# Folding two separate stages of an eight-core RWKV-style layer into the blocks beside them

## What is computed

```
xn = layernorm(x)
xx = shift(xn) - xn                                # the token before, minus this one
xk, xv, xr, xg = xn + xx * tm_k, tm_v, tm_r, tm_g
k = xk @ Wk.T;  v = xv @ Wv.T;  r = xr @ Wr.T;  g = sigmoid(xg @ Wg.T)
wkv = scan over tokens of (a + e^u e^k v) / (b + e^u e^k)
o = (sigmoid(r) * wkv * g) @ Wo.T
s = layernorm(o) * ln_g + ln_b
scale = mean(abs(Wf));  w_t = clip(round(Wf / scale), -1, 1)
g2 = silu(xn @ (w_t * scale).T + bias)
y = x + s * g2
```

## Time and profile before

| what | us |
|---|---|
| median of two timed runs (1721.29, 1731.93) | 1726.61 |
| the profiled execution, device time | 1707.37 |
| its span on the slowest core (3) | 1705.8 |
| spans of the eight cores | 1696.6 to 1705.8 |
| TensorE busy | 815.9 (48% of the span) |
| VectorE busy | 600.4 (35%) |
| ScalarE busy | 461.9 (27%) |
| mean granted TensorE clock, core 3 | 0.742 |

### The profile page before, as it was taken

How to read it: one execution, slowest core, us unless ns; L and a number is a source line. 1 busy time by engine, 2 the same in 40 slices (tenths; PEclk the granted TensorE clock), 3 DMA queues, 4 the chain that set the end, 5 groups by cost and what they waited for, 6 DMA issues and landing times. The chain is left out here.

```text
span 1705.8 us, 12040 instructions; the slowest of 8 cores (1696.6 to 1705.8 us)
## 1 busy us (share of the span) xinstructions
PE 815.9 (48%) x3834; PEld 363.1 (21%) x3834; DVE 600.4 (35%) x977; ACT 461.9 (27%) x605; POOL 118.1 (7%) x190
## 2 busy tenths in 40 slices
PE   0520000421494948999950767709466029884000
PEld 0100000000252424544420323304223014331000
DVE  0059993001101000467104454446553320001844
ACT  0810001421221212122112334443334422445400
POOL 0002221000010000001110000000000010000010
PEclk9955555555797978999985888859788559987555
DMA  6003333775526374465127444463544462300076
GB/s 196 27 32 129 144 146 141 258 230 176 174 108 188 120 250 142 144 220 176 59 77 226 128 131 135 131 198 111 166 134 142 121 165 70 116 1 0 0 252 240
DMA packets 86910, 238.91 MB, mean 140 GB/s; under 512 B 11584, under 2 KB 15680, under 8 KB 84800
## 3 DMA queue, kind: packets, MB, share of 16 engines
q1 hardware_dynamic: 52128, 139.57, 27.8%
q0 software_dynamic: 20896, 76.56, 13.0%
q10 hardware_dynamic: 13824, 22.03, 3.8%
HBM read 180.44 MB, written 53.48 MB: 137 GB/s over the span
## 5 line engine op out<-in xcount | busy, mean ns | idle before, releaser
L963 PE MATMUL rgo_ps<-mov_rg,rgo_wbf 128*128 128x512 bf16 x1024 | 237.6, 397 | 204.3 <-ACT rgo_wbf L780 67.0
L379 PE MATMUL g1ps<-mov_kv,g1wbf 128*128 128x512 bf16 (+1 forms) x1536 | 261.1, 335 | 140.1 <-ACT g1wbf L246 60.1
L780 ACT ACTIVATE rgo_wbf<-rgo_mw 128x512 bf16<-128x512 f32 x192 | 119.6, 629 | 309.1 <-DMA rgo_mw<-wr 111.4
L379 PEld LDWEIGHTS g1ps<-mov_kv,g1wbf 128*128 128x128 bf16 x1536 | 132.9, 101 | 268.2 <-issue 152.9
L963 PEld LDWEIGHTS rgo_ps<-mov_rg,rgo_wbf 128*128 128x128 bf16 x1024 | 103.2, 101 | 338.8 <-issue 228.6
L963 PE MATMUL rgo_ps<-wkv_sb,rgo_wbf 128*128 128x512 bf16 x512 | 117.5, 394 | 84.2 <-ACT rgo_wbf L780 76.6
L621 PE MATMUL ps_sc<-fs_a,ones 128*1 128x512 f16 x64 | 29.8, 621 | 216.9 <-ACT fs_a L609 216.9
L244 DVE CAST g1wbf<-g1mwstg 128x1024 bf16<-128x1024 f32 x32 | 22.2, 694 | 271.7 <-DMA g1mwstg<-wk 96.2
L379 PE MATMUL g1ps<-xn_sb,g1wbf 128*128 128x512 bf16 x512 | 112.4, 383 | 5.6 <-DVE g1wbf L241 5.6
L308 ACT ACTIVATE g1row<-g1ps 128x512 f32<-128x512 f32 (+1 forms) x96 | 44.8, 492 | 147.5 <-PE g1ps L379 132.6
L963 PEld LDWEIGHTS rgo_ps<-wkv_sb,rgo_wbf 128*128 128x128 bf16 x512 | 51.4, 101 | 150.3 <-issue 94.5
(11 more groups left out here) (120 smaller groups left out, 882.7 us busy)
## 6 DMA issues: line engine op xcount, KB each, us to landing
fs_w<-wf SPq DMA_DIRECT2D x16, 1024.0 KB, 6.0
g1mwstg<-wk SPq DMA_DIRECT2D x32, 512.0 KB, 5.2
g1mwstg<-wv SPq DMA_DIRECT2D x32, 512.0 KB, 5.1
g1mwstg<-wf SPq DMA_DIRECT2D x32, 512.0 KB, 4.7
rgo_mw<-wr SPq DMA_DIRECT2D x64, 256.0 KB, 3.5
rgo_mw<-wg SPq DMA_DIRECT2D x64, 256.0 KB, 3.4
rgo_mw<-wo SPq DMA_DIRECT2D x64, 256.0 KB, 3.2
x_sb<-x SPq DMA_DIRECT2D x16, 576.5 KB, 15.2
```

The source lines that it names most:

```text
L379: mm = e.matmul(bank[:, :t1 - t0], wbf[hh % 2][:, ic, oc * 128:(oc + 1) * 128], s["mov"][:, ic, t0:t1], start=(ic == 0), stop=(ic == CH - 1))
L780: e.activation(wbf[ss % 2][:, ic, :], mwstg[jj % 2][:, :], AF.Copy).then_inc(sem["scs"], 1)
L963: mm = e.matmul(bank[:, :t1 - t0], wbf[ss % 2][:, ic, oc * 128:(oc + 1) * 128], phs[p]["mov"][:, ic, t0:t1], start=(ic == 0), stop=(ic == ...
```

## The change

The scale stage loses its block. Its SP, ACT, PE and DVE work is written into block B of the first layer norm: SP's loads first thing there, ACT's and PE's part behind their broadcasts, DVE's five small operations behind its 16 chunks. Two semaphores are exchanged (`scv` for `ss`, `srd` for `sv`).

The last stage loses its block too. Its work is written into block B of the second layer norm. `s_sb` goes; ACT writes a double tile `sstg`, and DVE does the normalisation of chunk `ci`, then multiply and add of chunk `ci - 1`. The tiles for x, g2 and y are double as before.

Cut to its core:

```diff
@@ block B of the first layer norm
+            QC = _tchunks(C)
+            nbc = len(TC_STG)
@@ its tensor stream, behind the pb1 and pb2 matmuls
+                for ic in range(CH):
+                    e.wait_ge(sem["scv"], b["scv"] + ic + 1)
+                    for j, (q0, q1) in enumerate(QC):
+                        mm = e.matmul(ps_sc[:, :q1 - q0], ones16[:, :],
+                                      habs[ic % 2][:, q0:q1],
+                                      start=(ic == 0 and j == 0),
+                                      stop=(ic == CH - 1 and j == len(QC) - 1))
+                    inc(mm, "smm")
+                e.wait_ge(sem["srd"], b["srd"] + 1)
...
+            @blk.sync
+            def _(e):
+                for ic in range(CH):
+                    if ic >= 2:
+                        e.wait_ge(sem["scv"], b["scv"] + ic - 1)
+                    inc(e.dma_start(wstg[ic % 2][:, :],
+                                    w_d["wf"][ic * 128:(ic + 1) * 128, :]),
+                        "sw%d" % (ic % 2), 16)
@@ its scalar stream, behind rb_sb and m2b_sb
+                for ic in range(CH):
+                    swp = "sw%d" % (ic % 2)
+                    e.wait_ge(sem[swp], b[swp] + 16 * (ic // 2 + 1))
+                    if ic >= 2:
+                        e.wait_ge(sem["smm"], b["smm"] + nbc + ic - 1)
+                    inc(e.activation(habs[ic % 2][:, :], wstg[ic % 2][:, :],
+                                     AF.Abs), "scv")
+                e.wait_ge(sem["smm"], b["smm"] + nbc + CH + 1)
+                e.activation(scale_sb[:, :], ps_bc[:, 0:1], AF.Copy)
...
@@ its vector stream, behind the 16 chunks
+                e.wait_ge(sem["smm"], b["smm"] + nbc + CH)
+                e.tensor_copy(sctile[:, :], ps_sc[:, :])
...
+                inc(e.tensor_scalar(sctiny[:, 2:3], sctiny[:, 1:2], -1.0, None,
+                                    OP.mult), "srd")
@@ the scale stage's own block
-    with contextlib.ExitStack() as es:
...
@@ block B of the second layer norm
-    s_sb = s_es.enter_context(nc.sbuf_tensor("s_sb", [128, CH, T_OWN], F32))
+            @blk.sync
+            def _(e):
+                for ci in range(CH):
+                    if ci >= 2:
+                        e.wait_ge(sem["sden"], b["sden"] + ci - 1)
+                    inc(e.dma_start(xst[ci % 2][:, :],
+                                    x_d[ci * 128:(ci + 1) * 128,
+                                        1 + LANE:T_STG]),
+                        "sw%d" % (ci % 2), 16)
+                    inc(e.dma_start(g2ld[ci % 2][:, :], sg2[ci, :, :]),
+                        "sw%d" % (ci % 2), 16)
             @blk.scalar
                 for ci in range(CH):
                     e.wait_ge(sem["sv"], b["sv"] + ci + 1)
-                    inc(e.activation(s_sb[:, ci, :], ost[ci % 2][:, :],
+                    if ci >= 2:
+                        e.wait_ge(sem["sden"], b["sden"] + ci - 1)
+                    inc(e.activation(sstg[ci % 2][:, :], ost[ci % 2][:, :],
+            def final_part(e, ci):
+                swp = "sw%d" % (ci % 2)
+                e.wait_ge(sem["ss"], b["ss"] + ci + 1)
+                e.wait_ge(sem[swp], b[swp] + 32 * (ci // 2 + 1))
+                if ci >= 2:
+                    stp = "st%d" % (ci % 2)
+                    e.wait_ge(sem[stp], b[stp] + 16 * (ci // 2))
+                e.drain()
+                e.tensor_tensor(outst[ci % 2][:, :], sstg[ci % 2][:, :],
+                                g2ld[ci % 2][:, :], OP.mult)
+                e.drain()
+                inc(e.tensor_tensor(outst[ci % 2][:, :], outst[ci % 2][:, :],
+                                    xst[ci % 2][:, :], OP.add), "sden")
@@ its vector stream, in the loop over ci
                     inc(e.tensor_tensor(ost[ci % 2][:, :], ost[ci % 2][:, :],
                                         m2b2[:, :], OP.subtract), "sv")
+                    if ci >= 1:
+                        final_part(e, ci - 1)
+                final_part(e, CH - 1)
+            @blk.gpsimd
+            def _(e):
+                for ci in range(CH):
+                    e.wait_ge(sem["sden"], b["sden"] + ci + 1)
+                    inc(e.dma_start(y_d[ci, :, :], outst[ci % 2][:, :]),
+                        "st%d" % (ci % 2), 16)
...
@@ the last stage's own block
-    with contextlib.ExitStack() as es:
-        ec = es.enter_context
-        xst = [ec(nc.sbuf_tensor("xst%d" % i, [128, T_OWN], F32))
```

More of the change, by code:

```diff
@@ L509, in build_nc @@
             pb2 = ecB(nc.psum_tensor("pb2", [128, 512], F32))
+            SCW = min(512, C)
+            ps_sc = ecB(nc.psum_tensor("ps_sc", [1, SCW], F32))
+            ps_bc = ecB(nc.psum_tensor("ps_bc", [128, 4], F32))
+            wstg = [ecB(nc.sbuf_tensor("fs_w%d" % i, [128, C], F32))
+                    for i in range(2)]
+            habs = [ecB(nc.sbuf_tensor("fs_a%d" % i, [128, C], F16))
+                    for i in range(2)]
+            sctile = ecB(nc.sbuf_tensor("sctile", [1, SCW], F32))
+            sctiny = ecB(nc.sbuf_tensor("sctiny", [1, 4], F32))
             blk = esB.enter_context(nc.Block())
             b = snap()
+            QC = _tchunks(C)
+            nbc = len(TC_STG)
             @blk.tensor
@@ L564, in _ @@
                         "sv")
+                e.wait_ge(sem["smm"], b["smm"] + nbc + CH)
+                e.tensor_copy(sctile[:, :], ps_sc[:, :])
+                e.drain()
+                e.reduce_sum(sctiny[:, 3:4], sctile[:, :], axis=AX.X)
+                e.drain()
+                e.tensor_scalar(sctiny[:, 0:1], sctiny[:, 3:4], 1.0 / (C * C),
+                                None, OP.mult)
+                e.drain()
+                e.tensor_scalar(sctiny[:, 1:2], sctiny[:, 0:1], FFN_EPS, 0.5,
+                                OP.add, OP.mult)
+                e.drain()
+                inc(e.tensor_scalar(sctiny[:, 2:3], sctiny[:, 1:2], -1.0, None,
+                                    OP.mult), "srd")
             @blk.gpsimd
@@ L972, in build_nc @@
     o_sb = sr_sb
-    s_es = contextlib.ExitStack()
-    s_sb = s_es.enter_context(nc.sbuf_tensor("s_sb", [128, CH, T_OWN], F32))
     with contextlib.ExitStack() as es:
@@ L1049, in build_nc @@
             pb2 = ecB(nc.psum_tensor("qb2", [128, 512], F32))
+            sstg = [ecB(nc.sbuf_tensor("sstg%d" % i, [128, T_OWN], F32))
+                    for i in range(2)]
+            xst = [ecB(nc.sbuf_tensor("xst%d" % i, [128, T_OWN], F32))
+                   for i in range(2)]
+            g2ld = [ecB(nc.sbuf_tensor("g2ld%d" % i, [128, T_OWN], BF16))
+                    for i in range(2)]
+            outst = [ecB(nc.sbuf_tensor("outst%d" % i, [128, T_OWN], F32))
+                     for i in range(2)]
             blk = esB.enter_context(nc.Block())
             b = snap()
+            ntc2 = len(TC_OWN)
             @blk.tensor
```

118 lines of the change are left out of this document (13 added, 105 removed).

## The result

The changed kernel takes 1618.35 us (median of 11 runs, 1611.7 to 1627.6), the kernel before, run beside it, 1726.61 us (median of 10, 1706.1 to 1759.0). The ratio is 0.9445, 95% interval 0.9409 to 0.9481: faster by 5 to 6%. The forecast was 1610 us, the range 1588 to 1640. The time lies 8.4 us above the forecast and inside the range.

A forecast was written before the change was run, and what follows sets the result against it. Stages that leave idle what their neighbour needs stand one behind the other only because all engines meet between blocks. 75.1 + 39.3 - 3 = 111.4 us, taken from 1721.3, gives 1610 us; range 1588 to 1640.

The forecast's parts named there:

- The last stage, +39.3: Folded into the second layer norm's block B: 16 chunks of 5.30 us, last add at 1661.4 instead of 1700.7, gain 39.3 us.
- the slack of 0.7 and 0.9 us: Last stage: 8.07 us of DVE work was to cover g2's load (7.35 us) and y's store (7.16 us).
- The rival that it is not hidden: Last stage: x, g2 or y land too late and DVE waits in each pair; 1627 to 1649 us, chance 0.12.
- The tail of the scale, ACT and PE, 0: First layer norm's block B: DVE's five small operations have 9 us of cover, ACT and PE finish early; cost 0.
- The scale stage, 75.1 less 3: Folded into the first layer norm's block B: 75.07 us removed, less 3 us for stores and loads meeting at the DMA engines.
- The bound of 17 us: First layer norm's block B: upper limit of the stores' delay if `fs_w` loads always went first, 1.6 chunks late.
- The rival with the loads ahead of the stores: First layer norm's block B grows by up to 17 us as longer load rows win the DMA engines; 1624 us, chance 0.15.
- The middle, 0: Between the two edits, 1217.7 us before: no term; a change over 10 us would make the prediction wrong.
- M: Theory set up for the follow-up runs: the change really lengthens the middle, about 1221 us against 1214; no chance given.
- The base: Whole kernel: gain subtracted from 1721.3 us, the middle of three executions (1707.4, 1721.3, 1731.9); from the timed median, 1615.
- the stage is hidden, not moved: First layer norm's block B: rival that `fs_w` ends behind DVE, moving the scale stage; up to 1685 us, chance 0.02.
- the rival with the slow clock: Matmul phases: starting 75 us earlier, about 680 more matmuls at the low TensorE clock; chance 0.02 slower, 0.03 within 2%.

The follow-up runs named there:

- e1: The changed kernel with the end as before, so only the scale stage folded into block B; ratio 0.9599 against the kernel before.
- e2: The changed kernel with the scale stage in its own block as before, so only the last stage folded in; ratio 0.973 against the kernel before.
- e5: The changed kernel without the mean subtraction in the second layer norm, three DVE operations per chunk instead of four; last stage 80.1 us, one profiled execution.
- e4: The changed kernel loading only the first two pieces of `fs_w`, each used eight times by ACT and PE; ratio 0.937 against the kernel before.
- e3b: Second run of the changed kernel with `fs_w` loads paced one per DVE chunk, beside the changed kernel; ratio 0.9406 against the kernel before.
- e3: The changed kernel with each `fs_w` load issued only when DVE has finished the chunk two earlier; ratio 0.9323 against the kernel before.
- e6: The changed kernel with paced `fs_w` loads, three tiles each for x, g2 and y, and the last stage's first multiplication on POOL; ratio 0.9396.
- e8: The changed kernel with paced `fs_w` loads, three tiles each for x, g2 and y, and bf16 normalised output and statistics; ratio 0.9232.

## Why the prediction was right, and where it was off

- **The bound and the kind of gain: right.** All engines met between stages that used different ones, and both edits put one beside the other. e1 and e2 show each gain apart.
- **The last stage, +39.3: measured 38.3.** The pair of 2.53 us and the wait of 0.09 held. The wait taken at 0.15 was 0.08, which gave 16 x 0.07 = 1.1 us back; the slack of 0.7 and 0.9 us did not wholly hold, with landings of up to 8.0 us where at most 7.5 were forecast, and 2.6 us of waits in the mean. 84.8 - 1.1 + 2.6 = 86.3 us, measured 86.0 to 86.3: two small errors that nearly cancel. The rival that it is not hidden fell. e5 shows how thin the cover was: a chunk shorter by 1.31 us is already bound by landings.
- **The tail of the scale, ACT and PE, 0: right.** The last copy ends 9 us before the next block's first load, and e4 has DVE at its old pace beside ACT and PE.
- **The scale stage, 75.1 less 3: measured 63.7 (66.4 in the first pair of profiles).** The step that was off most: "That came through in 27 us beside the weight loads: a queue with a deep backlog is not starved. I take 3 us", from the `mov_kv` row. The waits measured 10 to 11 us in the mean and 3.2 to 16.5 by core. The bound of 17 us, worked out for loads that always go first, was all but reached on core 4. I read the wrong number in the right row. That 16 transfers with a backlog all get through says something about a queue's throughput; block B asks for the landing of one store within 7.35 us. The same row had that: a median of 10.5 us and a maximum of 14.3. With 10.5 each burst would have been 3.2 us late and the five bursts of that time 16 us. Measured were fewer and longer waits: three on core 4, 16.5 us in all. The rival with the loads ahead of the stores (1624 us, 14 us over the forecast) came about as near as the forecast: its extra loss over the 3 us was 7 to 8. Its rule, in the Trainium skill's "DMA: Bandwidth & Descriptors", section "Queues, rings and completion order", is that an engine takes turns between queues, a packet at a time; that the queue with the longer rows then gets more bytes was my inference from it. The waits have the direction that this gives, but their size is 10 to 11 us of the 17 that I worked out by it, and no run here shows single packets; e3b shows that the stores fall behind only while loads stand back to back.
- **The middle, 0: longer by 3.6 ± 1.6 us by the timed spans, by 7.6 in the profiles.** The prediction has no term for it and gives no reason why it should stay. The profiles show 1220 to 1227 us in the ten with the scale in block B that can be compared, 1218.4 in e2, and 1213.7 and 1215.4 in before. After less before is 7.5 and 7.6 us in the two pairs, under the 10 us at which I would have called the prediction wrong. e3 and e4 rule out that late stores cause it. The runs speak for M with a size of 4 to 8 us; a part of the pairs' difference comes from short executions of before, and the cause stays open.
- **The base, and some luck.** The gain was forecast as 111.4 us and measured as 98.4 in mean core span: 13.0 us too large, 8.4 in the scale stage, 1.0 in the last, 3.6 in the middle. That the time came out only 8.4 us above the forecast is owed to the base. I counted from 1721.3, the middle one of three executions; the executions of before that enter the ratio have a mean of 1713.9. From there the forecast would have been 1602.5, and 1618.35 is 16 us above it. (From the median of 1726.6 it would have been 1615, and seemingly better still.) The error of the base hid about half of the error of the gain.
- **The other rivals.** `fs_w` was done by 187 us, so the stage is hidden, not moved. The clock: 0.759 on core 3 where it was 0.742, over a span that lost about 100 us at 0.50. Nothing of the rival with the slow clock was seen at the size that it named; whether the clock has a part in the few microseconds of the middle stays open.

What the range owed to its width: the slowest core of eight alone moved 16 us between runs of the changed kernel.

## What to carry to other kernels

Two stages that leave each other's engines idle are worth laying side by side when a barrier is all that parts them; the gain is the shorter stage, less what they do to each other at the DMA engines. Price that contention with the landing time of a single transfer under load and the slack until it is wanted, not with throughput; and where the hidden loads have time, issue them one per burst of the other traffic instead of as fast as buffers come free. When two-deep buffers just cover a landing, one more tile is what the next shortening of the compute will need.

## What the runs showed of the hardware

- Beside back-to-back 1 MB loads, the last of five stores of 256 to 288 KB landed in up to 13.7 us on core 4, where it takes 3.4 to 3.6 alone and 7.3 beside one load per burst (e3b). Cores of one program differ widely in what it costs them: 3.2 to 16.5 us.
- With both queues working, the DMA engines moved 326 and 342 GB/s at a busy share of 0.99 and 0.98.
- A `tensor_tensor` on POOL took 2.15 us and drew DVE's fp32 operation beside it from 1.23 to 3.00 us (e6); that one ended 1.08 us after POOL's.
- The same 128x1024 `tensor_tensor` on DVE takes 1.23 us where the output and one input are fp32 and 0.69 us with all three in bf16 (e8).
- Less its waits, block B kept its length with ACT, PE and the loads beside it: 151.8 to 152.1 us in before, after and e4.
